# State space layers: the products that sum the step sizes ahead of a sum of states in TensorE's queue

## The reference, cut to what matters

```python
xz = jnp.einsum('bsd,ed->bse', x, in_w)
x_in, z = jnp.split(xz, 2, axis=-1)
xc = silu(causal_depthwise_conv(x_in) + cb)
dbl = jnp.einsum('bsd,ed->bse', xc, xp_w)     # 8 + 16 + 16 columns: dtr, Bm, Cm
dt = jax.nn.softplus(jnp.einsum('bsr,dr->bsd', dtr, dt_w) + dt_b)
A = -jnp.exp(A_log)
...
dA = jnp.exp(dt_t[..., None] * A)
h = h * dA + (dt_t * u_t)[..., None] * B_t[:, None, :]
y = jnp.einsum('bdn,bn->bd', h, C_t)
...
y = y + xc * Dp
y = y * silu(z)
return jnp.einsum('bse,de->bsd', y, out_w)
```

## Time and profile before

| | |
|---|---|
| device time, median of 3 runs | 2795.13 us (2794.46 to 2795.56) |
| the profiled execution, its own time | 2799.16 us |
| its span, first to last instruction | 2797.4 us |
| mean granted clock of TensorE, share of full speed | 0.962 |
| busy over the span: PE, DVE, ACT, POOL | 2505.2, 1938.2, 1702.8, 1145.3 us |
| the state space stage in the span | about 545 to 1444 us |
| costliest groups, all of this stage: POOL line 1309, DVE line 1242, PE line 1487, ACT line 1386 | 600.3, 576.7, 483.4, 425.0 us |

### The profile page before, as it was taken

The page is one execution under the profiler, slowest core; times in us unless marked ns, Lnnn a source line. Parts: engine busy times, 40 slices in busy tenths (PEclk is TensorE's granted clock), DMA queues, the critical chain, the costliest instruction groups (busy, mean ns, idle before and its releaser), DMA issues. The chain is left out here.

```text
span 2797.4 us, 38034 instructions
## 1 busy us (share of the span) xinstructions
PE 2505.2 (90%) x11190; PEld 1419.3 (51%) x11190; DVE 1938.2 (69%) x3923; ACT 1702.8 (61%) x3567; POOL 1145.3 (41%) x919
## 2 busy tenths in 40 slices
PE   7999978599999999999978899968879998799977
PEld 5766643245555454545533344446654444556655
DVE  6888855499999999999965444456653444577754
ACT  3565522399999999998943244347753443466634
POOL 1000011199999999999950000033210001254432
PEclk9999989799999999999999999979998998999988
DMA  2000023144444444344433211100002110000000
GB/s 103 1 1 1 1 92 83 62 149 154 152 152 151 152 152 156 150 158 149 153 151 80 76 61 61 61 1 1 0 1 100 67 61 27 1 1 0 1 1 16
DMA packets 34619, 205.64 MB, mean 74 GB/s; under 512 B 4000, under 2 KB 5152, under 8 KB 13216
## 3 DMA queue, kind: packets, MB, share of 16 engines
q1 hardware_dynamic: 34464, 203.83, 20.5%
HBM read 201.19 MB, written 2.62 MB: 73 GB/s over the span
## 5 line engine op out<-in xcount | busy, mean ns | idle before, releaser
L1309 POOL TENSOR_TENSOR mam_state_c<-mam_state,weights_r 128x1024 f32<-128x1024 f32 x256 | 600.3, 2363 | 58.8 <-DVE mam_state L1242 58.6
L1242 DVE TENSOR_TENSOR_SCAN mam_state<-banks,mam_dbu 128x1024 f32<-128x1024 f32 x256 | 576.7, 2273 | 0.6 <-ACT banks L1386 0.6
L1487 PE MATMUL banks<-mam_state_c,identity 128*128 128x512 f32 x1024 | 483.4, 604 | 26.4 <-POOL mam_state_c L1309 26.4
L1386 ACT ACTIVATE banks<-mam_dt,mam_a_neg 128x255 f32<-128x255 f32 x1024 | 425.0, 461 | 70.0 <-DVE mam_state L1242 69.1
L1487 PEld LDWEIGHTS banks<-mam_state_c,identity 128*128 128x128 f32 x1024 | 184.1, 190 | 225.1 <-issue 169.8
L1003 PE MATMUL banks<-route_xnt,weights_r 128*128 128x512 f32 x512 | 247.5, 608 | 8.1 <-PEq L67 8.1
L1225 DVE TENSOR_TENSOR mam_dbu<-banks,weights_r 128x1024 f32<-128x1024 f32 x192 | 227.5, 1198 | 6.8 <-ACT banks L1394 6.8
L556 POOL TENSOR_SCALAR route_ln_rs<-route_ln_mv 128x4 f32<-128x4 f32 x16 | 5.1, 320 | 495.2 <-DVE route_ln_mv L634 495.2
L436 ACT ACTIVATE at_probs<-banks,at_nmax 128x256 f32<-128x256 f32 x256 | 118.0, 473 | 140.0 <-DVE at_nmax L377 140.0
L2504 POOL TENSOR_TENSOR at_attention<-at_relu 128x512 f32<-128x512 f32 x128 | 131.2, 1042 | 127.9 <-ACT at_relu L2549 80.3
L957 DVE TENSOR_TENSOR m2a_hidden<-m2a_gelu,m2a_comb_spread 128x512 f32<-128x512 f32 x120 | 80.7, 689 | 116.4 <-ACT m2a_gelu L983 113.7
(11 more groups left out here) (435 smaller groups left out, 5116.7 us busy)
## 6 DMA issues: line engine op xcount, KB each, us to landing
weights_r<-mam_bc_rows SPq DMA_DIRECT2D x128, 1024.0 KB, 4.6
m2a_comb_spread<-m2a_comb_rows SPq DMA_DIRECT2D x15, 1024.0 KB, 8.2
m2b_comb_spread<-m2b_comb_rows SPq DMA_DIRECT2D x15, 1024.0 KB, 7.1
m1a_comb_spread<-m1a_comb_rows SPq DMA_DIRECT2D x14, 512.0 KB, 7.3
m1b_comb_spread<-m1b_comb_rows SPq DMA_DIRECT2D x14, 512.0 KB, 7.5
weights_r<-in_mb SPq DMA_DIRECT2D x1, 4332.0 KB, 12.9
weights_r<-in_m SPq DMA_DIRECT2D x1, 4200.0 KB, 12.8
weights_r<-in_a SPq DMA_DIRECT2D x1, 2632.0 KB, 12.9
```

Of the source, the lines that this page charges most:

```text
L1242: dve.tensor_tensor_scan(flat2(h[:, i % 4, :, :, :]), decay(i), flat2(dbu[:, i % 4, :, :, :]), 0.0, ALU.mult, ALU.add).then_inc(h_ready, 1)
L1309: pool.tensor_tensor(hc[:, j % 4, :, :, :], h[:, j % 4, :, :, :], c_rows(j), ALU.mult).then_inc(hc_ready, 1)
L1386: i = act.activation(decay(j)[:, o + 1:o + S], dt[:, q, c, 1:S], ACT.Exp, scale=aneg[:, l, k:k + 1])
L1487: k = pe.matmul(y_bank(q)[:, :], K.ident[:, :], flat(hc[:, j % 4, n, :, :]), start=(j == 0 and n == 0), stop=(j == NP - 1 and n == 1))
```

## The change

TensorE's `step_sizes` is called right behind `prepare` in the slot, ahead of the sum of states, where it was called behind the sum. Only slot 4 is touched, since `step_sizes` does nothing in other slots. The queues of the other engines are the same, and so are the table loads of ScalarE.

```diff
                 def slot(i, now, last, nxt, after):
                     prepare(i, nxt, after)
+                    step_sizes(i, nxt)
                     at = lagged(i, 2, NP, now, last)
                     if at:
                         l, s, q, j = at
@@
                             for c in range(C):
                                 pe.matmul(y_bank(q)[:, c * S:(c + 1) * S], skip[:, l, c, :], xc[:, q, c, :],
                                           start=False, stop=False)
-                    step_sizes(i, nxt)
                     if not now and i == 2:
                         route_tensor(K, ahead, pe, 0, "xt")
```

## The result

| | before | with the change |
|---|---|---|
| device time, median | 2794.8 us (4 runs) | 2750.7 us (4 runs) |
| ratio | | 0.9846, 95% interval 0.9821 to 0.987 |
| the same, measured again with more runs | 2793.85 us (9 runs) | 2750.33 us (5 runs), 0.9844, 0.9829 to 0.9859 |
| the profiled execution's span | 2797.4 us | 2742.9 us |
| first to last `hc` of pair 0 in the span | 859.0 us | 815.8 us |

The kernel is 44 us faster, 1.5%; the interval lies clear of 1. 2752.0 us was forecast.

A forecast was written before the change was run, and what follows sets the result against it. Bound: a closed hand-over loop of 27.61 us a unit, with VectorE waiting on TensorE's queue. At 26.32 us, 31 units take 815.9 instead of 859.0 us; the 43.1 us gain off 2795.13 gives 2752.0 us, range 2746 to 2763.

The forecast's parts named there:

- The wait goes because sum 2 stands no longer in front of the last product: TensorE slot 4: the loop loses sum 2's 1.72 us, 27.61 to 25.89 us; VectorE's 1.42 us wait at line 1217 goes.
- TensorE's loop there: Last layer, with its longer output: TensorE's loop falls from 28.05 to 26.33 us a unit, as long as the two-unit loop.
- The three products come ahead of sum 2 without a stop for the logarithm: TensorE slot 4: the logarithm's product would start at 818.13, its input ready at 816.80, so 1.33 us to spare.
- Sum 2 costs nothing in its new place: TensorE: sum 2, 2.58 us later, fills time waited anyway before line 152's transpose of the normalised rows; cost zero.
- a loop over two units through GpSimd, ScalarE and VectorE: State space stage: parts of 19.46, 7.94, 22.88 and 2.35 us sum to 52.63 us over two units, 26.32 us each.
- VectorE alone: Rival: the two-unit loop has hidden slack and VectorE's own 26.19 us a unit sets the pace; 2748 us, chance 0.15.
- The wait at line 1217: Sign: VectorE's wait for TensorE's line 1475 product before the dt addition gone, or below 0.3 us, in units 1 to 31.
- TensorE's wait for `hc` 1: Sign: TensorE still waits for GpSimd's product `hc` 1, some 0.3 to 0.4 us.
- VectorE's waits for decays at scan 1: Sign: small VectorE waits for ScalarE's decays (line 1386) at scan 1 in every second unit.
- Half of it back: Rival: late decays at scan 1 or 5, or slower GpSimd products, cost 0.6 us a unit; 2771 us, chance 0.12.
- The slower case: Rival: a late logarithm stops TensorE's queue; addition later than before from 3.05 us lateness; 2806 us at 3.4, chance 0.04.
- A table load without a drain: ScalarE function switches: 1.28 us load only, against the skill's added 1.38 us drain, which would make 31 us a unit.

The follow-up runs named there:

- ahead_of_output: Changed kernel with the three step size products moved further forward, behind sum 1 but ahead of the last unit's output products; 2752.69 us in one run.
- pool_short: Changed kernel without GpSimd's negation of the mean in the layer norm (line 1286), its sign left out of the computation; 2741.4 us in one run.
- ahead_of_sum_1: Changed kernel with the three step size products moved to slot 3, ahead of sum 1 and the output products; 2787.43 us in one run.
- act_ahead_of_copy: Changed kernel with two small extra ScalarE activations a unit, placed ahead of the input copy and its wait for GpSimd's product; 2753.15 us in one run.
- log_last: Changed kernel with only the logarithm's step size product put back behind sum 2; 2791.44 us, 0.9999 of the kernel before the change.

## Why the prediction was right, and where it was not

*The wait goes because sum 2 stands no longer in front of the last product.* Right, and shown: the wait is gone with the change and back at 1.42 us when only the last product is put back. In the last layer 0.11 to 0.15 us of it is left at units of 26.34 us, as was said of TensorE's loop there (26.33 us).

*The three products come ahead of sum 2 without a stop for the logarithm.* Right. 1.33 us to spare were read from the rows; 0.96 us are left with the change (830.45 to 831.41), since ScalarE has moved against TensorE by a few tenths. `ahead_of_output` used this up and stopped for 0.27 us.

*Sum 2 costs nothing in its new place, because TensorE waits there for the normalised rows.* Right: it waits 0.41 us behind sum 2, and 2.2 us when sum 2 is taken out of this time. The prediction added that up to 1.7 us of lost cover would touch line 152 "but not for the scans". No run makes the normalised rows come sooner, so that this case is not tested as it stands. But work of the same 1.72 us put behind the transpose made the units 1.6 us longer at full clock: what stands there, the convolution and the sums, feeds ScalarE, and the loop through it had only some 0.1 us to spare.

*The new period is set by a loop over two units through GpSimd, ScalarE and VectorE, 26.32 us.* Right in size, 815.78 / 31 = 26.32 us, and in kind as far as it can be told: added work on its ScalarE part costs half of itself and in every second unit; beside the loop it costs next to nothing. That the mean meets 26.32 us to the last digit is partly luck. The forecast took one pair of units for all, while before they were 27.6 us in one half of a layer and 27.7 us in the other, and with the change the distances from one `hc` 0 to the next go from 26.16 to 26.47 us. In the changed kernel the alternation is there in the second layer but small:

```profile
648.61 0.66 DVE L1217 TENSOR_TENSOR mam_dt<-banks,mam_dt_relu 128x512 f32<-128x512 f32 x1
...
674.90 0.66 DVE L1217 TENSOR_TENSOR mam_dt<-banks,mam_dt_relu 128x512 f32<-128x512 f32 x1
...
701.29 0.66 DVE L1217 TENSOR_TENSOR mam_dt<-banks,mam_dt_relu 128x512 f32<-128x512 f32 x1
...
727.55 0.66 DVE L1217 TENSOR_TENSOR mam_dt<-banks,mam_dt_relu 128x512 f32<-128x512 f32 x1
```

26.29, then 26.39 and 26.26 us. The loop lies only 0.1 us over VectorE's own time, so "VectorE alone" at 2748 us was nearly as good a description; the measured 2750.7 us lies between it and the forecast. Only `pool_short` tells the two apart, by 2.0 us. GpSimd's own queue is as close: without its waits for scan 0 its units are 26.15 to 26.23 us, and these waits come to 0.1 us a unit in the mean. That they are there at all speaks for the loop, and so does the wait at scan 1, which goes with it (`pool_short`). So three bounds lie within 0.15 us, and with them the one of TensorE and ScalarE at an estimated 26.20 us.

*What would show it.* ScalarE's wait for `dt_u` was forecast at 0.8 us and is 0.82; the transpose waits for ScalarE as said. The wait at line 1217 was to stay under 0.3 us in units 1 to 31; it does but for the last addition, 0.89 us. TensorE's wait for `hc` 1 was forecast at 0.3 to 0.4 us; the row of sum 1 at 826.53 carries none. VectorE's waits for decays at scan 1 are there, but too short to be listed, 0.08 us in the mean, and they come in nearly every unit, the longer ones mostly in every second.

*The rivals.* Half of it back: no; line 1309 takes 2364 ns in the middle where it took 2361, with GpSimd in nearly constant use, so that no hindrance between VectorE and GpSimd shows here. The Trainium skill's rule (SBUF — State Buffer, section SBUF: two separate sides), by which VectorE and GpSimd exclude each other when VectorE reads two operands from SBUF, left no ground for it, since VectorE's scans read one of theirs from a bank. The rows agree; no run here has the other case. The slower case did not occur, but `ahead_of_sum_1` made it by hand. The prediction had it begin when the addition comes later than before; there the addition comes with no wait for TensorE in any unit but the last, and the kernel loses all the same, over the loop that TensorE's stopped queue closes with ScalarE. The mechanism was named rightly and its onset placed too late.

*A table load without a drain.* The changed kernel packs ScalarE to where 1.38 us more for each of four switches could not be hidden: 25.26 us busy in 26.26. The logarithm ends at 830.45, the load starts at 830.47 and the decays at 831.77. As in the kernel before, the trace disagrees with the figure of the Trainium skill (ScalarE: Activation LUTs, section What ACT_TABLE_LOAD costs).

## What to carry to other kernels

Where several engines are each over 90% busy, follow the hand-overs round to the same instruction of the next unit. The parts of any such path add up to the period; the path that sets it is the one without slack, on which every part is work that begins as soon as the part before has ended. Ask which work lies on it only because of its place in a queue; that work can be moved by its full length into a wait elsewhere in the same queue. Then work out the next loop, also those that close over two rounds, since it sets what is gained: here 1.72 us were taken from one loop and 1.4 us a unit arrived (43.2 / 31). A product can be put too far forward: once it waits for its input, it holds back all that stands behind it, and between two nearly full engines that wait comes back again.

## What the runs showed of the hardware

A pause of TensorE that is costly for the clock can be short. With sum 2 behind the transpose TensorE stood 2.21 to 2.31 us once a unit in units 0 to 24 (2.48 us in unit 0), in a stage where it is busy for over 85% of the time. In nine of these 25 units the work behind the pause ran partly at 1.2 GHz: sums 2 and 3 took 5.06 to 5.29 us. In the other sixteen they took 3.60 us, after pauses of the same length. In units 25 to 29, where the pause is 1.76 to 1.86 us, none shows it. The nine are units 3, 5, 8, 11, 13, 16, 19, 21 and 24: each the second or the third from the one before, in the order 2, 3, 3, so that they are not picked at random. This is one execution, and what sets the order is open.

The rest of the kernel, which no experiment changed, took from 1923 to 1938 us in the profiled executions (span less the stage: before 1938.4, changed 1927.1, changed again 1925.2, `ahead_of_output` 1934.3, `act_ahead_of_copy` 1935.1, `ahead_of_sum_1` 1923.3). A part of it is the start of the two stages of the expert layers before and behind the third mixer. The first 27 us of the first of them, before and then with the change (columns as above):

```profile
1583.00:1595.00 12.00, 11.68 (x17) 4.55 (x18) 2.48 (x4) 3.92 (x5) 0.00 (x0) 0.64 0.66 262
1595.00:1610.00 15.00, 15.00 (x31) 6.08 (x30) 5.41 (x15) 4.12 (x6) 1.27 (x2) 0.86 0.01 3
...
1538.00:1550.00 12.00, 10.90 (x21) 4.46 (x22) 2.48 (x4) 3.92 (x5) 0.00 (x0) 0.86 0.55 212
1550.00:1565.00 15.00, 15.00 (x36) 6.31 (x35) 7.71 (x20) 5.50 (x8) 1.27 (x2) 1.00 0.10 43
```

Before, TensorE has 0.64 and then 0.86 of its clock there; with the change, 0.86 and 1.00. The second of these stages shows the same (0.63 and 0.90; 0.83 and 1.00). The whole of such a stage, from the first to the last activation of line 983, took 238.5 and 238.4 us in the one and 234.5 and 234.2 us in the other, which is 8 of the 9.8 us behind the stage. Since `log_last`, as slow as before in its stage, has the short form as well (234.1 us), and `ahead_of_output`, as fast as the change, has a long one (238.6 us for its second), it is not the change that brings it. I do not know what decides it. For comparing two kernels of this kind the time between two instructions of the stage in question is the better measure: it came out 0.1 us apart in the two profiles of the changed kernel, where the rest of the kernel moves by up to 15 us.
